# Causal masks of an attention's score maxima: two mask products that split the diagonal block by keys in place of queries

## The chip, the cores and the metric

The kernel runs on one core of one Trainium2 chip. The metric is device time in microseconds, from runs of the whole program, shown as a median with its lowest and highest value. One further execution is profiled; all rows below are from that one.

## The reference

Two layers on x of shape (2, 2048, 256). The first adds a differential attention and a mixture of experts, the second a state-space block and a sign-weight network. The change touches the attention alone:

```python
q, k, v = jnp.split(x @ w_attn, 3, axis=-1)       # 32 maps of 8 columns each, in pairs: 16 heads
att = jnp.einsum('bhtd,bhsd->bhts', q, k) * (1.0 / math.sqrt(hd))   # q scaled by hd ** -0.5 before
att = jnp.where(causal, att, -jnp.inf)
att = jax.nn.softmax(att, axis=-1)
att = att.reshape(B, H, 2, T, T)
att = att[:, :, 0] - lambda_full * att[:, :, 1]
out = jnp.einsum('bhts,bhsd->bhtd', att, v)       # then a norm, gamma and a projection
```

The softmax needs, for each query, the maximum over the keys up to and including its own.

## The kernel before

**Stages.** Norm, q/k/v and routing; the experts; the attention; the projection; the state-space and sign-weight stage. The tables of this change are made by GpSimd in the experts' stage (`phase_experts`, lines 782 to 791) and used in the attention's (`phase_attention`).

**Attention.** 32 heads (2 batches of 16), each with two maps a = 0 and 1. Map a has its q and k in rows 64a to 64a+63 of the slabs `qslab` and `kslab` (q and k are cut into bf16 parts, 48 rows in all), so a product of one map uses half of TensorE's rows and can run beside one of the other map. For each head there are

- 70 *maximum items* (`max_items`, numbered 0 to 69, even ones map 0, odd ones map 1). An item is one PSUM bank of up to 512 columns: products of 128 queries with up to 512 keys (L1374, `max_products`), for some a mask (L1388, `max_mask`), then one reduction on VectorE (L1322, `take_max`) into `pmax`. 48 items are full blocks of 512 keys. 22 are masked, since their last 128 keys are the queries' own (the diagonal block): items 2 and 3 hold four query tiles with 128 keys each; 8, 9, 14 and 15 hold two with 256 keys each; 22, 23, 28, 29, 34, 35, 40, 41, 46, 47, 54, 55, 60, 61, 66 and 67 hold one, with 384 or 512 keys.
- one transpose of the finished maxima (L1396), copied by ScalarE, cut by GpSimd into three bf16 rows and brought by DMA to rows 48 to 50 of `qslab`, so that the score product already subtracts the maximum.
- 40 *steps* of scores (L1426), exponentials on ScalarE (L1268), the causal cut on GpSimd where needed (L1200), and value products in f32 (L1441), which are issued for two steps at once.
- 4 *folds* (L1402): eight f32 records of 34 columns that sum the row groups.

**Order.** Items, transposes and folds share a ring of three PSUM banks, `psR`. Item number at in the ring may start only when what stood three places before it was read (`ring_free`). The order on every engine is written out: `place_items` spreads a head's items over the steps, most of them during the head before. TensorE takes all in program order, step by step: the first item's products, the two score products, that item's mask, the remaining fills, and at every second step the value products of two earlier steps. So whatever waits for a bank holds up all that is behind it.

**The mask.** It is added by accumulating products of `ident_b` (weights, rows to queries) with `mask_q` (0 or -1e30) onto the last 128 columns of each of the item's tiles. The items of one map may use 64 rows of the array only, so the 128 x 128 triangle takes two products of 64 rows. Before, product `part` adds the mask of queries 64 part to 64 part + 63, over all 128 keys: `ident_b[rows, part]` puts row r at query r + 64 part, and `mask_q[rows, part]` holds 128 keys. `mask_q` is read again for each tile of the item by a broadcast.

Of the kernel before, what the change touches and what calls it, by code (L numbers as in the profile page):

```python
# [6 lines left out]
BF16 = mybir.dt.bfloat16  # L7
# [4 lines left out]
ALU = mybir.AluOpType  # L12
AX = mybir.AxisListType

P = 128
# [15 lines left out]
NEG = -1e30  # L31
# [605 lines left out]
def phase_experts(nc, io, keep, dram):  # L637
# [4 lines left out]
    with ExitStack() as ctx:  # L642
# [3 lines left out]
        sem = lambda name: credited(ctx, nc, sems, name)  # L646
        MT = M // P
        HALF = P // 2
        SLABS = 2
        kslabs, qslabs = keep["kslabs"], keep["qslabs"]  # L650
        ident_b, mask_q, fold, lam_in, lam_s = (keep[x] for x in ("ident_b", "mask_q", "fold", "lam_in", "lam_s"))
# [69 lines left out]
        def _(sp):  # L721
# [22 lines left out]
            k_rows = dram["k"].rearrange("b n x d t -> (b n) x d t")  # L744
            sp.wait_ge(early_made, 2 * SLABS + 2 + CREDIT)
            for n in range(SLABS):
                for a in range(2):
                    row, lo = 2 * n + a, HALF * a
                    for at_, count, part in ((0, 3, 0), (3, 2, 1), (5, 1, 2)):
# [5 lines left out]
            for a in range(2):  # L755
                row, lo = a, HALF * a
                for at_, count, part in ((0, 3, 0), (3, 2, 1), (5, 1, 2)):
# [3 lines left out]
            for s in range(2):  # L761
                sp.wait_ge(y_out[s], 16 * (RT // 2) + CREDIT)
            for n in range(SLABS):
                sp.wait_ge(slab_in[n], 192 + CREDIT)

        @block.gpsimd
        def _(pool):
            c = Chain(pool, early_made)
            c.wait()
            for n in range(SLABS):  # L770
                for a in range(2):
                    c.mark(pool.memset(kslabs[n][HALF * a + 32:HALF * a + HALF, :], 1.0))
            c.wait()
            for a in range(2):
                c.after(pool.memset(qz[a][:], 0.0))
            c.after(pool.memset(ident_m[:], 0.0))
            c.after(pool.memset(mask_m[:], 0.0))
            c.after(pool.affine_select(out=ident_m[:], in_=ident_m[:], compare_op=ALU.not_equal, fill=1.0, base=0,
                                       pattern=[[-1, P]], channel_multiplier=1))
            c.after(pool.affine_select(out=mask_m[:], in_=mask_m[:], compare_op=ALU.is_ge, fill=NEG, base=0,  # L780
                                       pattern=[[-1, P]], channel_multiplier=1))
            c.after(pool.memset(ident_b[:], 0.0))
            c.after(pool.memset(mask_q[:], 0.0))
            c.after(pool.memset(fold[:], 0.0))
            for a in range(2):
                rows = slice(HALF * a, HALF * a + HALF)
                for part in range(2):
                    c.mark(pool.affine_select(out=ident_b[rows, part], in_=ident_b[rows, part], compare_op=ALU.not_equal,
                                              fill=1.0, base=HALF * part, pattern=[[-1, P]], channel_multiplier=1))
                    c.mark(pool.affine_select(out=mask_q[rows, part], in_=mask_q[rows, part], compare_op=ALU.is_ge,  # L790
                                              fill=NEG, base=HALF * part, pattern=[[-1, P]], channel_multiplier=1))
            c.wait()
            for odd in range(2):
                c.after(pool.affine_select(out=fold[:], in_=fold[:], compare_op=ALU.not_equal, fill=1.0,
                                           base=-VW * odd, pattern=[[-2 * VW, 2], [-1, OC]], channel_multiplier=1))
# [161 lines left out]
def phase_attention(nc, io, keep, dram):  # L957

    with ExitStack() as ctx:
# [23 lines left out]
        HALF = P // 2  # L983
# [3 lines left out]

        SLABS = 2
        ident_b, mask_q, fold, lam_s = (keep[x] for x in ("ident_b", "mask_q", "fold", "lam_s"))
# [368 lines left out]
        def _(pe):  # L1358
# [21 lines left out]
            def max_mask(n, x):  # L1380
                a, parts, masked = ITEMS[x]
                if not masked:
                    return
                w = parts[0][2]
                dst = psR[PLACE[("max", n, x)] % BANKS][:, 0:len(parts) * w].rearrange("p (m w) -> p m w", w=w)
                rows = slice(HALF * a, HALF * a + HALF)
                for part in range(2):
                    ins = pe.matmul(dst[:, :, w - P:w], ident_b[rows, part],  # L1388
                                    mask_q[rows, part].unsqueeze(1).to_broadcast([HALF, len(parts), P]),
                                    start=False, stop=(part == 1), skip_group_check=True)  # L1390
                ins.then_inc(ring_full, 1)

            def turn_max(n):
# [1090 lines left out]
def build(nc, io, out):  # L2484
    with ExitStack() as ctx:
# [13 lines left out]
        keep = {  # L2499
            "ident": sb(ctx, "ident", [P, P]),  # L2500
            "conv_w": sb(ctx, "conv_w", [P, CT, NTAP]),
            "vec": sb(ctx, "vec", [P, 3, CT]),
            "a_log": sb(ctx, "a_log", [P, CT, NS]),
            "a_neg": sb(ctx, "a_neg", [P, CT, NS]),
            "scal": sb(ctx, "scal", [P, 3]),
            "fac": sb(ctx, "fac", [P, 4]),
            "later_in": ctx.enter_context(nc.semaphore("later_in")),
# [5 lines left out]
        with ExitStack() as attn:  # L2513
            keep["c"] = sb(attn, "c_all", [P, NBLK, 2 * TPB])
            keep["yslot"] = sb(attn, "yslot_all", [P, NBLK, 2 * TPB], I32)
            keep["v"] = sb(attn, "v_all", [P, BATCH, HEADS, ST_T, VD])
            with ExitStack() as moe:
                keep["hot"] = sb(moe, "hot_all", [P, NBLK, 2, TPB, E])
                keep["slot"] = sb(moe, "slot_all", [P, NBLK, 2 * TPB])
                keep["table"] = sb(moe, "table", [P, 2, RT], I32)  # L2520
                keep["wg"] = sb(moe, "wg", [P, NE, KD, M])
                keep["wu"] = sb(moe, "wu", [P, NE, KD, M])
                keep["wd"] = sb(moe, "wd", [P, NE, M // P, D])
                phase_norm_qkv(nc, io, keep, dram)
                side = lambda name, shape, dt: early.enter_context(nc.sbuf_tensor(name, shape, dt, side="right"))
                keep["kslabs"] = [side(f"kslab{u}", [P, T], BF16) for u in range(2)]
                keep["qslabs"] = [side(f"qslab{u}", [P, T], BF16) for u in range(2)]
                keep["ident_b"] = side("ident_b", [P, 2, P], BF16)
                keep["mask_q"] = side("mask_q", [P, 2, P], BF16)
                keep["fold"] = side("fold", [P, 2, OC], F32)  # L2530
                keep["lam_in"] = side("lam_in", [P, 4, HD], F32)
                keep["lam_s"] = side("lam_s", [P, 2], F32)
                keep["pmax"] = side("pmax", [P, 2, ST_T, BPB], F32)
                keep["early_in"] = [early.enter_context(nc.semaphore(f"b_slab_in{u}")) for u in range(2)]
                phase_experts(nc, io, keep, dram)
            keep["o"] = sb(attn, "o_all", [P, NH, ST_T, VD])
            keep["raw_in"] = sb(attn, "raw_in", [P, ET, D])
            keep["raw_out"] = sb(attn, "raw_out", [P, KD, DI])
            keep["raw_x"] = sb(attn, "raw_x", [XD, DI])
            keep["raw_dt"] = sb(attn, "raw_dt", [P, CT, RANK])  # L2540
            keep["k0"] = sb(attn, "k0", [P, 2 * KD, F1], U8)
            keep["k1"] = sb(attn, "k1", [P, FT, F1], U8)
            keep["k2"] = sb(attn, "k2", [P, FT, D], U8)
            keep["wp"] = sb(attn, "wp", [P, KD, D])
            keep["gamma"] = sb(attn, "gamma", [P, 1])
            phase_attention(nc, io, keep, dram)
            early.close()
            keep["winT"] = far("winT", [P, KD, 2 * DI])
            keep["woutT"] = far("woutT", [P, CT, D])
            keep["wxT"] = far("wxT", [P, CT, XD])  # L2550
            keep["wdtT"] = far("wdtT", [RANK, DI])
            keep["w0"] = far("w0", [P, KD, F1], F16)
            keep["w1"] = far("w1", [P, FT, F1], F16)
            keep["w2"] = far("w2", [P, FT, D], F16)
            keep["skip"] = far("skip", [P, CT, P // 2])
            keep["taps"] = far("taps", [P, CT, NTAP, P])
            keep["xT"] = far("xT_s", [P, KD, BLK])
            keep["x1"] = far("x1_s", [P, TPB, D])
            phase_project(nc, io, keep, dram)
# [35 lines left out]
```

## Time and profile before

| | us |
|---|---|
| median of 3 runs | 3709.15 |
| lowest and highest | 3707.5, 3710.26 |
| profiled execution, its own time | 3713.02 |
| its span, from the first instruction to the last | 3711.3 |

The profile names engines PE (TensorE's products), PEld (its weight loads), DVE (VectorE), ACT (ScalarE) and POOL (GpSimd). A row of a group gives line, engine, operation, output and inputs, the shape, the count, busy time and the mean duration of one; then how long the engine had been idle before these instructions, and what ended it. The duration of one product runs until its last column has left the array, and the next product can follow before that, so durations overlap.

### The profile page before, as it was taken

How to read it: one execution, taken by the hardware profiler on the slowest of the kernel's cores; microseconds unless marked ns; L12 is line 12 of the kernel's file. 1: busy time of each engine (PE TensorE's matmuls, PEld its weight loads, DVE VectorE, ACT ScalarE, POOL GpSimd, SP SyncE). 2: the span in 40 equal slices, each digit the busy share in tenths (PEclk: the TensorE clock that was granted, in tenths of full speed). 3: DMA queues.
4: the chain of work that ended last, by engine and by line, in shares of the span. 5: the costliest groups of instructions: out<-in, count | busy, mean ns of one | idle time of the engine just before them, and what ended most of it. 6: DMA issues, size and time to landing. Idle time of an engine off the chain costs nothing. (4 is left out here: it accounts for less than half of the span.)

```text
span 3711.3 us, 61145 instructions
## 1 busy us (share of the span) xinstructions
PE 3425.7 (92%) x20658; PEld 1454.4 (39%) x20671; DVE 2739.1 (74%) x4434; ACT 2219.3 (60%) x3461; POOL 1499.4 (40%) x1843
## 2 busy tenths in 40 slices
PE   8996999989999999999999999767998998989987
PEld 5563666643333333333333333342333333333332
DVE  4653223468888888888888888265889888888888
ACT  3331221137777777777777777637767756667663
POOL 1212000013323333333233333215778777777786
PEclk9997999989999999999999999888999999999988
DMA  4443111111111011111100110031222222122221
GB/s 150 142 137 97 45 45 44 42 34 39 49 40 32 28 34 33 33 33 32 32 28 28 30 33 24 25 130 52 68 65 72 71 66 72 63 74 70 63 72 53
DMA packets 159224, 211.69 MB, mean 57 GB/s; under 512 B 30658, under 2 KB 106698, under 8 KB 158938
## 3 DMA queue, kind: packets, MB, share of 16 engines
q1 hardware_dynamic: 142042, 174.47, 15.6%
q10 hardware_dynamic: 10752, 16.78, 1.4%
q0 software_dynamic: 6144, 16.79, 1.4%
q8 instruction: 160, 2.62, 0.3%
q14 instruction: 126, 1.03, 0.1%
HBM read 154.48 MB, written 52.69 MB: 56 GB/s over the span
## 5 line engine op out<-in xcount | busy, mean ns | idle before, releaser
L1322 DVE TENSOR_REDUCE pmax<-psR 128x1 f32<-128x512 f32 (+3 forms) x2170 | 1321.5, 669 | 184.0 <-PE psR L1374 98.2
L1268 ACT ACTIVATE prob<-psS 128x1024 f32<-128x1024 f32 (+3 forms) x1280 | 1099.5, 904 | 364.2 <-PE psS L1426 360.8
L2081 POOL TENSOR_TENSOR hc<-h_d,crep 128x512 f32<-128x512 f32 x512 | 649.0, 1272 | 253.8 <-DVE h_d L2295 203.7
L1374 PE MATMUL psR<-kslab,qslab 48*128 48x512 bf16 (+3 forms) x2480 | 679.4, 353 | 38.7 <-DVE pmax L1322 10.9
L1426 PE MATMUL psS<-qslab,kslab 51*128 51x512 bf16 (+3 forms) x2560 | 646.7, 352 | 6.3 <-ACT prob L1268 4.3
L1441 PE MATMUL psVo<-prob,vaug 128*32 128x512 f32 (+3 forms) x5120 | 627.1, 545 | 0.9 <-ACT ov L1272 0.9
L1200 POOL TENSOR_SCALAR_AFFINE_SELECT prob<-prob 128x256 f32<-128x256 f32 (+1 forms) x512 | 208.8, 420 | 806.8 <-ACT prob L1268 806.5
L2295 DVE TENSOR_TENSOR_SCAN h_d<-a,state,psU 128x512 f32<-128x512 f32 x384 | 489.4, 1275 | 0.0
L2285 DVE TENSOR_TENSOR psU<-dtx,psX 128x512 f32<-128x512 f32 x512 | 356.1, 696 | 165.4 <-PE psX L2439 102.6
L1374 PEld LDWEIGHTS psR<-kslab,qslab 48*128 48x128 bf16 x2480 | 185.3, 94 | 726.2 <-DVE pmax L1322 512.6
L2203 ACT ACTIVATE a<-dt,a_neg 128x512 f32<-128x512 f32 x512 | 364.8, 720 | 54.5 <-DVE h_d L2295 53.1
L2456 PE MATMUL psYd<-hc,ident 64*64 64x512 f32 x2048 | 291.7, 641 | 7.9 <-POOL hc L2081 7.9
L2408 PE MATMUL psW<-f1h,w 128*128 128x512 f16 x512 | 195.4, 382 | 5.6 <-ACT xs L2134 3.9
L2408 PE MATMUL psW<-f1l,w 128*128 128x512 f16 x512 | 194.3, 380 | 0.0
L804 ACT ACTIVATE sg<-psG 128x512 f32<-128x512 f32 x72 | 43.0, 598 | 252.2 <-PE psU L896 252.2
L1173 POOL MEMSET kslab<- 32x2048 bf16 x4 | 7.2, 1798 | 461.8 <-SPq L1107 461.7
L1388 PE MATMUL psR<-mask_q,ident_b 64*128 64x512 bf16 (+1 forms) x1364 | 192.7, 241 | 0.0
L1426 PEld LDWEIGHTS psS<-qslab,kslab 51*128 51x128 bf16 x2560 | 158.2, 94 | 57.5 <-ACT prob L1268 33.9
L841 DVE COPY xT_e<-psX 128x256 f32<-128x256 f32 x72 | 30.3, 421 | 201.5 <-PE psX L883 201.5
L2295 DVE TENSOR_TENSOR_SCAN h_d<-a,psU 128x512 f32<-128x512 f32 x128 | 155.4, 1214 | 0.0
L275 POOL DMA_INDIRECT rows_d<-xn,slot x64 | 64.3, 1004 | 225.5 <-DVE slot L360 208.4
L1441 PEld LDWEIGHTS psVo<-prob,vaug 128*32 128x32 f32 x5120 | 102.3, 108 | 128.7 <-issue 88.6
(286 smaller groups left out, 4847.4 us busy)
## 6 DMA issues: line engine op xcount, KB each, us to landing
crep<-c_rows_d SPq DMA_DIRECT2D x256, 256.0 KB, 3.2
x_e<-rows_d SPq DMA_DIRECT2D x72, 128.0 KB, 2.0
y_d<-y SPq DMA_DIRECT2D x72, 128.0 KB, 1.7
q_d<-parts SPq DMA_DIRECT2D x48, 128.0 KB
k_d<-parts SPq DMA_DIRECT2D x48, 128.0 KB
qslab<-q_d SPq DMA_DIRECT2D x64, 96.0 KB
kslab<-k_d SPq DMA_DIRECT2D x64, 96.0 KB
x<-in_L_attn_x_dram SPq DMA_DIRECT2D x8, 512.0 KB, 6.0
```

The source lines that it names most:

```text
L1200: pool.affine_select(out=region, in_=region, compare_op=ALU.is_ge, fill=0.0, base=BLK * c + off - P * st, pattern=[[0, 2], [1, w]], channe ...
L1268: act.activation(prob[g % BUFS][:, :, off:BLK], psS[g % 2][:, :, off:BLK], ACT.Exp).then_inc(prob_ready, 1)
L1322: dve.tensor_reduce(pmax[:, a].rearrange("p i c -> p (i c)")[:, lo:lo + (count - 1) * NEXT + 1:NEXT], psR[at % BANKS][:, 0:count * w].rear ...
L1374: ins = pe.matmul(dst[:, m * w:(m + 1) * w], qslab[u][rows, i * P:(i + 1) * P], kslab[u][rows, ch * BLK:ch * BLK + w], start=(m == 0), sto ...
L1426: ins = pe.matmul(psS[g % 2][:, a, off:BLK], kslab[u][rows, st * P:(st + 1) * P], qslab[u][rows, c * BLK + off:(c + 1) * BLK], start=True, ...
L1441: ins = pe.matmul(psV[lo:lo + VW, off:BLK], vaug[n % 2][:, st, :], prob[g % BUFS][:, a, off:BLK], start=(st < 2), stop=(st >= TPB * c + TP ...
L2081: pool.tensor_tensor(hc[:, g % CR], h[:, g % HR], crep[:, g // PAIR % SPR], ALU.mult).then_inc(hc_ready, 1)
L2203: act.activation(a[:, g % AR], dt_[:, c], ACT.Exp, scale=a_neg[:, c, s:s + 1]).then_inc(a_ready, 1)
L2285: dve.tensor_tensor(psU[g % 2][:], dtx[:, c], psX[g // PAIR % 2][:], ALU.mult).then_inc(u_ready, 1)
L2295: dve.tensor_tensor_scan(h[:, g % HR], a[:, g % AR], psU[g % 2][:], 0.0 if blk % BPB == 0 else state[:, c, s:s + 1], ALU.mult, ALU.add).th ...
L2408: ins = pe.matmul(dst[:], ops[n][0], ops[n][1], start=(n == 0), stop=(n == OPS[kind] - 1))
L2456: ins = pe.matmul(psY[half][HALF * m:HALF * m + HALF, :], ident[rows, rows], hc[rows, (PAIR * k + m) % CR], start=False, stop=(s == NS - 1 ...
```

## The change

Each of the two products now covers 64 keys of a diagonal block in place of 64 queries. Product 0 adds the mask of keys 0 to 63: only queries 0 to 62 need one, row r for query r. Product 1 adds that of keys 64 to 127: row r for query r + 64 with r up to 62 (query 127 sees all keys), and the row that is left over, 63, masks all 64 keys for queries 0 to 63. So `mask_q` holds 64 keys for each part in place of 128, its row 63 of part 1 is -1e30 throughout, and `ident_b` has in row 63 of part 1 a one for queries 0 to 63 and a zero for query 127. Each product streams 64 columns for each tile in place of 128. Weights stay 64 rows of 128 columns, and the number of products stays. GpSimd makes the tables with six more selects, and with waits between them.

```diff
+        BIG = 1024
...
             for a in range(2):
                 rows = slice(HALF * a, HALF * a + HALF)
+                last = HALF - 1
                 for part in range(2):
-                    c.mark(pool.affine_select(out=ident_b[rows, part], in_=ident_b[rows, part], compare_op=ALU.not_equal,
-                                              fill=1.0, base=HALF * part, pattern=[[-1, P]], channel_multiplier=1))
+                    c.after(pool.affine_select(out=ident_b[rows, part], in_=ident_b[rows, part], compare_op=ALU.not_equal,
+                                               fill=1.0, base=HALF * part, pattern=[[-1, P]], channel_multiplier=1))
                     c.mark(pool.affine_select(out=mask_q[rows, part], in_=mask_q[rows, part], compare_op=ALU.is_ge,
-                                              fill=NEG, base=HALF * part, pattern=[[-1, P]], channel_multiplier=1))
+                                              fill=NEG, base=0, pattern=[[-1, HALF]], channel_multiplier=1))
+                c.wait()
+                c.after(pool.affine_select(out=ident_b[rows, 1], in_=ident_b[rows, 1], compare_op=ALU.is_ge,
+                                           fill=1.0, base=BIG * last - HALF, pattern=[[1, P]], channel_multiplier=-BIG))
+                c.after(pool.affine_select(out=ident_b[rows, 1], in_=ident_b[rows, 1], compare_op=ALU.not_equal,
+                                           fill=0.0, base=BIG * last + P - 1, pattern=[[-1, P]], channel_multiplier=-BIG))
+                c.after(pool.affine_select(out=mask_q[rows, 1], in_=mask_q[rows, 1], compare_op=ALU.is_ge,
+                                           fill=NEG, base=last - 1, pattern=[[0, HALF]], channel_multiplier=-1))
...
                 for part in range(2):
-                    ins = pe.matmul(dst[:, :, w - P:w], ident_b[rows, part],
-                                    mask_q[rows, part].unsqueeze(1).to_broadcast([HALF, len(parts), P]),
-                                    start=False, stop=(part == 1), skip_group_check=True)
+                    lo = w - P + HALF * part
+                    ins = pe.matmul(dst[:, :, lo:lo + HALF], ident_b[rows, part],
+                                    mask_q[rows, part].unsqueeze(1).to_broadcast([HALF, len(parts), HALF]),
+                                    start=False, stop=True, skip_group_check=True)
...
-                keep["mask_q"] = side("mask_q", [P, 2, P], BF16)
+                keep["mask_q"] = side("mask_q", [P, 2, P // 2], BF16)
```

## Rows read from the trace of the kernel before

**Rows 1.** Page, costliest groups of the whole span.

```profile
L1322 DVE TENSOR_REDUCE pmax<-psR 128x1 f32<-128x512 f32 (+3 forms) x2170 | 1321.5, 669 | 184.0 <-PE psR L1374 98.2
...
L1388 PE MATMUL psR<-mask_q,ident_b 64*128 64x512 bf16 (+1 forms) x1364 | 192.7, 241 | 0.0
```

**Rows 2.** Windows, ten heads: length, each engine's busy us, clock, DMA.

```profile
1000.00:1500.00 500.00, 485.89 (x4018) 175.09 (x4016) 438.45 (x739) 375.32 (x496) 157.53 (x315) 1.00 0.13 38
```

**Rows 3.** Waits in 1000 to 1500: us in all, times, longest.

```profile
PEld psR L1374 <- DVE pmax L1322: 167.0, 293, 0.8
...
ACT prob L1268 <- PE psS L1426: 113.3, 193, 1.1
...
DVE pmax L1322 <- PE psR L1374: 31.5, 92, 0.7
DVE pmax L1322 <- PE psR L1388: 27.1, 50, 1.0
```

**Rows 4.** Tile psR in 800 to 2300: min, median, max ns, first and last start.

```profile
L1396 PE MATMUL psR<-ident,nmax x30: 283/284/284, 844.2 to 2278.3; 128*32 128x128 f32 x30
```

**Rows 5.** Groups by form, PE, the masks' products of the whole span.

```profile
L1388 PE MATMUL psR<-mask_q,ident_b 64*128 64x128 bf16 x992 | 107.1, 216 | 0.0
...
L1388 PE MATMUL psR<-mask_q,ident_b 64*128 64x256 bf16 x248 | 48.0, 273 | 0.0
...
L1388 PE MATMUL psR<-mask_q,ident_b 64*128 64x512 bf16 x124 | 37.6, 383 | 0.0
```

**Rows 6.** Groups by form, weight loads in 1000 to 1500.

```profile
L1402 PEld LDWEIGHTS psR<-fold,ov 128*128 128x128 f32 x320 | 38.7, 191 | 14.6 <-issue 13.5
L1388 PEld LDWEIGHTS psR<-mask_q,ident_b 64*128 64x128 bf16 x442 | 37.2, 95 | 20.2
L1441 PEld LDWEIGHTS psVo<-prob,vaug 128*32 128x32 f32 x1624 | 32.2, 108 | 39.7 <-issue 27.0 <-ACT prob L1268 6.6
```

**Rows 7.** Timeline, items 22 and 23: start us, us, what [idle before it].

```profile
1401.42 0.22 PE L1388 MATMUL psR<-mask_q,ident_b 64*128 64x128 bf16 x1
...
1401.48 0.22 PE L1388 MATMUL psR<-mask_q,ident_b 64*128 64x128 bf16 x2
...
1401.73 2.82 DVE L1322 TENSOR_REDUCE pmax<-psR 128x1 f32<-128x384 f32 x5 [0.16 <-PE psR L1388]
```

**Rows 8.** Timeline, items 2 and 3 with the fold and the transpose.

```profile
1434.78 1.89 DVE L1322 TENSOR_REDUCE pmax<-psR 128x1 f32<-128x512 f32 x3
...
1434.89 0.59 PE L1388 MATMUL psR<-mask_q,ident_b 64*128 64x512 bf16 x2
...
1435.62 1.05 PE L1402 MATMUL psR<-fold,ov 128*128 128x34 f32 x8
...
1437.06 0.59 PE L1388 MATMUL psR<-mask_q,ident_b 64*128 64x512 bf16 x2
...
1437.58 0.28 PE L1396 MATMUL psR<-ident,nmax 128*32 128x128 f32 x1
1437.68 1.29 DVE L1322 TENSOR_REDUCE pmax<-psR 128x4 f32<-128x512 f32 x2 [1.01 <-PE psR L1388]
```

**Rows 9.** Timeline, items 8 and 9.

```profile
1440.19 0.38 PE L1388 MATMUL psR<-mask_q,ident_b 64*128 64x256 bf16 x2
...
1440.50 1.06 PE L1441 MATMUL psVo<-prob,vaug 128*32 128x512 f32 x8
...
1442.36 1.29 DVE L1322 TENSOR_REDUCE pmax<-psR 128x2 f32<-128x512 f32 x2 [0.66 <-PE psR L1388]
```

**Rows 10.** Timeline, item 35 and the value products behind it.

```profile
1408.88 0.27 PE L1388 MATMUL psR<-mask_q,ident_b 64*128 64x128 bf16 x2
1409.09 0.16 PEld L1441 LDWEIGHTS psVo<-prob,vaug 128*32 128x32 f32 x8
1409.09 1.06 PE L1441 MATMUL psVo<-prob,vaug 128*32 128x512 f32 x8
```

**Rows 11.** Timeline, load of a score product behind items 54 and 55.

```profile
1425.82 0.10 PEld L1426 LDWEIGHTS psS<-qslab,kslab 51*128 51x128 bf16 x2 [0.23 <-ACT prob L1268]
```

**Rows 12.** Timeline of GpSimd, the last mask select and what follows it.

```profile
326.79 0.29 POOL L790 TENSOR_SCALAR_AFFINE_SELECT mask_q<-mask_q 64x128 bf16<-64x128 bf16 x1
327.22 0.60 POOL L794 TENSOR_SCALAR_AFFINE_SELECT fold<-fold 128x34 f32<-128x34 f32 x2
```

## The prediction

> **What bounds the kernel now.** I read the page first. The masks' products at L1388 are 1364 records inside the attention stage, and the reductions they feed, L1322, are the largest group of the page [rows 1]. The question is whether that stage waits for TensorE. The windows view of 500 us in its middle gives PE 486 us busy, VectorE 438 and ScalarE 375 at a granted clock of 1.00 [rows 2]. "Busy" on PE includes the part of a product after its last column has entered, so 97% doesn't mean full. The waits of the same window say more: weight loads of the maxima's products wait 167.0 us for VectorE's reductions, and reductions wait 31.5 us for those products and 27.1 us (50 times) for the masks [rows 3]. So it is a ring of three PSUM banks in which now PE waits for VectorE, now VectorE for PE. ScalarE waits 113.3 us for scores, so it is rarely the bound. One head takes 49.45 us: 30 transposes of maxima start between 844.2 and 2278.3 us, 29 periods [rows 4]. The window holds ten heads, so VectorE waits five times a head for a mask, always at the same items, since the timeline repeats itself head by head.
>
> An average over waits does not tell what a shorter mask is worth, so I followed one head (1398.7 to 1448.1 us) through the timeline backwards: from a reduction that waited, to PE's product; along PE, until a product that itself began about 0.06 us after a reduction's end (a fold product 0.15 us after); along VectorE again. The saving counts only where that chain runs through a mask.
>
> **The change, part by part.**
>
> *The products.* There are 22 masked items a head, two products each: 16 items with one diagonal block, 4 with two, 2 with four. The streamed columns fall from 128, 256, 512 to 64, 128, 256. What a column costs: the record is 216, 273 and 383 ns [rows 5], about 0.43 ns a column on a fixed part; and one product follows the other in the same rows after 0.22 us at 512 columns (0.59 us for two less 0.38 for one), 0.11 at 256 (0.38 less 0.27), 0.06 at 128 (start 1401.42, then 1401.48) [rows 5, 7, 8, 9]. That is the streaming time and about 4 ns. So halving saves, for an item's two products: 2 x (0.217 - 0.110) = 0.21 us with four blocks, 2 x (0.110 - 0.057) = 0.107 with two, 2 x (0.057 - 0.030) = 0.054 with one. The first two go by paces that the trace shows. The 0.030 for 64 columns does not occur in it. Its bounds: 0.030 if streaming still sets the pace, 0.057 if something fixed (the weight load, which isn't shortened) does. The rows lean to 0.030: an f32 load of 128 columns is recorded at 191 ns and one of 32 at 108, thus 0.86 ns a column on 80 ns; the bf16 load is 95, which leaves 15 ns for the load proper [rows 6]. The fold's products show what such a load does when it sets the pace: eight in 1.05 us with some 0.28 for one is 0.11 us each for 34 columns, which is 128 x 0.86 ns [rows 8]. With 15 ns the load still hides under 27 ns of streaming. I take 0.030.
>
> The Trainium skill ("TensorE: Matmul & The Clock Gate", LDWEIGHTS) gives a load as columns / 1.2 ns, 107 ns for 128, and "it's the 128 columns that matter". By that, masks would go at 107 ns a product and the 64-column ones gain nothing. The trace contradicts it for bf16 (0.06 us a product with a load each) and agrees for f32 (0.11).
>
> *Which masks lie on the chain.* Item numbers are those of the list of 70.
> - Item 3 (four blocks). Mask to 1437.65, the transpose at 1437.58 right behind it, the values, then item 5's product; VectorE had stood 1.01 us for it [rows 8]. On the chain: 0.21.
> - Item 2 (four blocks). Its mask began at 1434.89, but the fold behind it started at 1435.62, 0.15 us after a reduction that freed its bank (the first of the three that start at 1434.78); by PE alone it could have started about 0.2 us earlier (the mask's streaming ends at 1435.32, and other products follow a mask 0.1 us behind it, as at item 35 [rows 8, 10]). VectorE sets it, so nothing: this 0.21 is lost.
> - Items 8, 9, 15 (two blocks). 8: the values start at 1440.50, right behind the second product; 9: VectorE stood 0.66 us for it [rows 9]; 15 as 8. 3 x 0.107 = 0.32.
> - One block: 22 (VectorE stood 0.16 us [rows 7]), 28 and 29 (side by side on the two halves of the rows, so once), 35 (values at 1409.09 right behind [rows 10]), 41, 66 and 67 (alike). 6 x 0.054 = 0.32, less 0.01 because VectorE had only about 0.09 us to spare at 67.
> - Items 54, 55: the chain behind them runs to a score product that waits 0.23 us for ScalarE [rows 11], whose work began ahead of these masks. Nothing.
> - The other eight (14, 23, 34, 40, 46, 47, 60, 61) end while VectorE has a backlog, and PE next waits for a bank. Nothing.
>
> Sum: 0.21 + 0.32 + 0.31 = 0.84 us a head. The first head's early items run alone before any scores, and the last head's period has no maxima, so 30 periods: 25 us. The waits allow this: VectorE stands (500 - 438) / 10 = 6 us a head [rows 2].
>
> *The set-up.* GpSimd gets six more selects of about 0.29 us and waits between them, some 2 us, after a last mask select at 326.79 [rows 12]. Nobody needs these tables before the attention stage, over 400 us on; GpSimd has only the fold's select behind them. In the path it would cost 2 us. The smaller mask tile moves its neighbours by 256 bytes, and both products now carry the stop flag: nothing.
>
> The sum against the profiled execution: 3713.0 - 25 = 3688. The median of the runs shown is 3.9 us below that execution, so 3709.15 - 25 = 3684 us.
>
> **Rivals.**
> 1. *The fixed part of a short product sets the pace (0.057).* One-block masks gain nothing, the others as above: 0.21 + 0.32 = 0.53 us a head, 16 us, 3693. For it: no 64-column product is in the trace, and both the load and the issue stay. Against: the load's 15 ns [rows 6]. The Trainium skill ("TensorEngine Tiling (Array Packing)", Instruction Overhead) has a floor of about 60 cycles a product, which 64 columns just clear; no row shows it.
> 2. *More than the chain.* Streamed time also helps where I wrote nothing: item 2, 54/55 and the backlog ones shift the pattern. All 22 would be 2 x 0.21 + 4 x 0.107 + 16 x 0.054 = 1.71 us a head, 52 us, 3657; with item 2 alone 1.05, 32 us, 3677. Against: PE waits for banks 167 us in 500, so most of what it gains off the chain it waits away.
> 3. *VectorE swallows it.* It is busy 438 of 500; if it gets a backlog earlier and the chain moves onto it, the saving returns as longer waits of PE for banks. Within 7 us if less than 0.24 us a head survives, about 3706. Against: at item 3 VectorE stands 1.01 us and at item 9 0.66, far above what is taken.
> 4. *Slower: unhidden loads.* If a load and its wait don't overlap a product this short, the pace could rise to the fold's 0.11 us. One-block items on the chain then lose 6 x 2 x (0.110 - 0.057) = 0.64 us, two-block ones gain nothing, item 3 keeps 0.21: +0.43 us a head, 13 us slower, 3722. It decides from a pace of about 0.10 us, where 12 x (pace - 0.057) passes 0.53. Against: two loads now follow at 0.06 us.
>
> **The numbers.** Forecast (gain 20 to 30 us) 0.52; rival 1 (10 to 20) 0.18; rival 2 (30 to 50) 0.17; rival 3 (under 7.4 either way) 0.09; rival 4 0.04. A difference of 0.2% (7.4 us) is about what a measurement can tell. Faster 0.87, same 0.09, slower 0.04. The range takes in rivals 1 and 2: 3660 to 3700.
>
> **What the changed profile would show.** Masks at 64, 128 and 256 columns with records near 188, 216 and 273 ns; two one-block products 0.03 us apart (rival 1: 0.06). Transposes of maxima 48.6 us apart in place of 49.45. VectorE's wait at item 3 near 0.8 us and at item 9 near 0.55; its waits on the masks down from 27.1 to about 22 us in 500. PE's waits for banks about as before (rival 3: up by what is saved). All other stages as long as now. I am wrong if the loads pace the short products, or if a place where I saw slack carries the chain once the masks before it are shorter.

## The result, and the profile after

Six runs of the changed kernel have a median of 3685.1 us (3683.3 to 3695.8), six of the kernel before 3709.7 us. The ratio is 0.9937, 95% interval 0.9927 to 0.9947: 20 to 27 us less. The prediction was 3684, 25 us less.

The profiled execution took 3683.5 us, its span is 3681.7. Lines have moved: products 1383, masks 1398, transpose of maxima 1406, folds 1412, scores 1436, values 1451, reductions 1331.

**The masks' products.** Groups by form on PE, whole span; they answer to [rows 5]:

```profile
L1398 PE MATMUL psR<-mask_q,ident_b 64*128 64x64 bf16 x992 | 87.3, 189 | 0.0
...
L1398 PE MATMUL psR<-mask_q,ident_b 64*128 64x128 bf16 x248 | 34.3, 218 | 0.0
L1398 PE MATMUL psR<-mask_q,ident_b 64*128 64x256 bf16 x124 | 24.0, 273 | 0.0
```

The same counts, half the columns; 189 ns is the 188 that the slope of [rows 5] gave. What matters is how closely they follow each other. The timeline of PE in the changed kernel, at items 22 and 23 as in [rows 7]:

```profile
1389.41 0.33 PE L1383 MATMUL psR<-kslab,qslab 48*128 48x384 bf16 x1
...
1389.57 0.19 PE L1398 MATMUL psR<-mask_q,ident_b 64*128 64x64 bf16 x1
...
1389.60 0.19 PE L1398 MATMUL psR<-mask_q,ident_b 64*128 64x64 bf16 x1
...
1389.63 0.22 PE L1398 MATMUL psR<-mask_q,ident_b 64*128 64x64 bf16 x2
```

Two products of item 22 start 0.03 us apart where 0.06 stood before, and the two of item 23 last 0.22 us together, 0.03 more than one. Start times are given to 0.01 us, so the 0.030 rests on both readings agreeing. It is what 64 columns at 0.42 ns and 4 ns of gap give: streaming still sets the pace, and the load stays hidden.

**The pace of a head.** Tile psR, transposes of maxima: count, min, median, max ns, first and last start. First the kernel before over its whole stage, then the changed one:

```profile
L1396 PE MATMUL psR<-ident,nmax x32: 283/284/372, 791.0 to 2325.7; 128*32 128x128 f32 x32
```

```profile
L1406 PE MATMUL psR<-ident,nmax x32: 284/284/372, 789.4 to 2298.9; 128*32 128x128 f32 x32
```

From first to last 1534.7 us became 1509.5: 25.2 us less over 31 periods. This length, called the *stage length* below, is the sharpest measure of the experiments, since noise elsewhere stays out of it. Each is read from one profiled execution; two kernels were profiled twice, and each pair agrees within 0.3 us. Within 1000 to 1500 us ten transposes start at 1042.0 to 1487.0 before and 1036.4 to 1473.9 after, so a steady head went from 49.44 to 48.61 us, 0.83 less; 0.84 was predicted.

**The waits.** The changed kernel, 1000 to 1500 us, answering to [rows 3]:

```profile
PEld psR L1383 <- DVE pmax L1331: 176.7, 303, 0.8
ACT prob L1277 <- PE psS L1436: 105.1, 185, 1.1
...
DVE pmax L1331 <- PE psR L1383: 31.3, 93, 0.7
...
DVE pmax L1331 <- PE psR L1398: 20.4, 41, 0.8
```

VectorE waits 6.7 us less for masks and as long as before for other products. The loads of the maxima's products wait 9.7 us more for VectorE, but that is mostly a change of label: the waits of the same loads that the profile puts under "issue" (nothing seen that they wait for) fell by 8.5. Before and after:

```profile
PEld psR L1374 <- issue: 60.0, 82, 0.8
```

```profile
PEld psR L1383 <- issue: 51.5, 73, 0.8
```

Nor is it what PE saves off the chain. The experiment e2 below, where only the masks on the chain are short, has the same two numbers (176.8 and 51.5); e3, where only the others are short, has 167.4 and 59.5, as before.

What PE saves at item 2 can be seen in one place. The fold behind it now shows a wait for VectorE, which it did not before:

```profile
1422.82 0.38 PE L1398 MATMUL psR<-mask_q,ident_b 64*128 64x256 bf16 x2
1423.55 1.05 PE L1412 MATMUL psR<-fold,ov 128*128 128x34 f32 x8 [0.35 <-DVE pmax L1331]
```

From the mask's start to the fold's it is 0.73 us, as in [rows 8] (1434.89 to 1435.62), though the mask is 0.21 us shorter.

**Item 3**, PE and VectorE in the timeline, answering to [rows 8]:

```profile
1424.99 0.38 PE L1398 MATMUL psR<-mask_q,ident_b 64*128 64x256 bf16 x2
...
1425.30 0.28 PE L1406 MATMUL psR<-ident,nmax 128*32 128x128 f32 x1
1425.41 1.29 DVE L1331 TENSOR_REDUCE pmax<-psR 128x4 f32<-128x512 f32 x2 [0.80 <-PE psR L1398]
```

From the start of the mask to the transpose it is 0.31 us in place of 0.52, and VectorE stands 0.80 us in place of 1.01. Both are the 0.21 of the sum.

### The profile page after: what moved, and what is told of

Read it like the earlier page. It is cut to its first block and busy times, and to the rows that moved or that the text cites. A ratio compares the mean times of both kernels' runs of the same rounds, so it can differ in the third digit from the quotient of the medians.

```text
span 3681.7 us, 61156 instructions
## 1 busy us (share of the span) xinstructions
PE 3381.3 (92%) x20658; PEld 1448.4 (39%) x20671; DVE 2735.0 (74%) x4434; ACT 2217.7 (60%) x3461; POOL 1501.7 (41%) x1849
## 5 line engine op out<-in xcount | busy, mean ns | idle before, releaser
L850 DVE COPY xT_e<-psX 128x256 f32<-128x256 f32 x72 | 30.3, 421 | 201.0 <-PE psX L892 201.0
L1412 PE MATMUL psR<-fold,ov 128*128 128x34 f32 x1024 | 136.0, 278 | 11.3 <-DVE pmax L1331 10.6
```

## The experiments

Each kernel is the changed one with one edit, run against the kernel before on the same chip. The stage length is read as above; the one of before is always that of its one profile (1534.7), which was not taken again beside the experiments. e1_wide, another execution that should equal it, is 0.1 away.

| kernel | median us | ratio to before, interval | stage length, us | less before's 1534.7 |
|---|---|---|---|---|
| changed | 3685.1 | 0.9937 [0.9927, 0.9947] | 1509.5 | -25.2 |
| e1_wide | 3712.7 | 1.0009 [0.9999, 1.0018] | 1534.8 | +0.1 |
| e2_on_chain | 3685.9 | 0.9938 [0.9921, 0.9954] | 1510.5 | -24.2 |
| e3_off_chain | 3710.9 | 1.0003 [0.9993, 1.0012] | 1534.0 | -0.7 |
| e4_item3 | 3702.3 | 0.9979 [0.9969, 0.9989] | 1528.3 | -6.4 |
| e5_four_of_32 | 3704.4 | 0.9984 [0.9974, 0.9993] | 1529.2 | -5.5 |
| e6_mask_first | 3679.1 | 0.9910 [0.9893, 0.9926] | 1504.2 | -30.5 |
| e7_no_masks | 3659.7 | 0.9857 [0.9840, 0.9873] | 1483.9 | -50.8 |
| e8_cut_22_28 | 3695.0 | 0.9963 [0.9950, 0.9976] | 1520.3 | -14.4 |
| e9_cut_rest | 3695.6 | 0.9961 [0.9946, 0.9977] | 1518.3 | -16.4 |
| after_again | 3684.5 | 0.9936 [0.9922, 0.9949] | 1509.2 | -25.5 |
| mask_first_again | 3677.5 | 0.9915 [0.9901, 0.9928] | 1504.4 | -30.3 |

**Which columns count: e1 to e4.** All four keep the changed kernel's split by keys, its stop flags and its way of making the tables. `mask_q` is 128 keys wide again, with zeros in the half that a product doesn't mask, so that a product can stream 64 keys or all 128 with the same result:

```diff
+        NARROW = (3, 8, 9, 15, 22, 28, 29, 35, 41, 66, 67)      # e2; e1: none; e3: the other 11; e4: (3,)
...
-                    lo = w - P + HALF * part
-                    ins = pe.matmul(dst[:, :, lo:lo + HALF], ident_b[rows, part],
-                                    mask_q[rows, part].unsqueeze(1).to_broadcast([HALF, len(parts), HALF]),
+                    at, cols = (HALF * part, HALF) if x in NARROW else (0, P)
+                    lo = w - P + at
+                    ins = pe.matmul(dst[:, :, lo:lo + cols], ident_b[rows, part],
+                                    mask_q[rows, part, at:at + cols].unsqueeze(1).to_broadcast([HALF, len(parts), cols]),
```

What was expected of e1, e2, e3 and e4, in this order:

> The new tables and the new split by keys, but every mask product streams all 128 keys of a diagonal block (64 of them against zeros). If the saving is the streamed columns on the chain, this is the kernel before: a head takes 49.45 us from transpose to transpose, the whole 3709 us, VectorE waits 27 us in 500 for the masks. If the split itself, the disjoint columns, the stop flags or the tables had part in it, it stays below, towards 48.6 us a head and 3685.

> Only the 11 items that the prediction put on the chain (3, 8, 9, 15, 22, 28, 29, 35, 41, 66, 67) stream 64 keys of a block, the other 11 stream 128. By the chain all of the gain is here: 48.6 us a head, 3685 us. If the gain is spread over all masks by their columns (rival 2), these 11 have 0.21 + 0.32 + 0.43 = 0.96 of 1.71 us, 56% of it: 0.5 of the measured 0.885 us, 48.95 us a head, 3695.

> Only the 11 other items (2, 14, 23, 34, 40, 46, 47, 54, 55, 60, 61) stream 64 keys of a block. By the chain nothing: 49.45 us a head, 3709 us, though PE streams 0.75 us less a head than before. Spread by columns: 0.39 us less, 49.06 us a head, 3697.

> Only item 3 (four blocks, map 1) streams 64 keys of a block. By the chain 0.21 us a head: 49.24 us, 6.4 us in all, 3703, VectorE's wait for it 0.80 in place of 1.01 us. If VectorE swallows it (rival 3): 49.45 and 3709.

Measured: e1 is the kernel before, so the split, the flags and the tables are worth nothing that shows; the saving is the streamed columns. e2 has 24.2 of the 25.2 us, e3 has 0.7. e4 has 6.4, what the chain gave for it (0.21 us x 31 is 6.5).

The two expectations for a spread by columns have a slip. The 11 items of e2 hold seven items with one block, not eight, so their share is 0.21 + 0.32 + 0.38 = 0.91 of 1.71 us, 53%, and PE streams 0.80 us less in e3, not 0.75; and the measured gain is 0.83 us a head, not 0.885. The spread would thus have given 13 us in e2 and 12 in e3. Neither is near what was measured.

In e3 the masks of 9 of the 16 one-block items and of items 2 and 14 are short, and VectorE still stands the full time at items 9 and 3, as these two groups show (VectorE by form, 1000 to 1500 us, e3):

```profile
L1333 DVE TENSOR_REDUCE pmax<-psR 128x2 f32<-128x512 f32 x40 | 26.6, 686 | 6.6 <-PE psR L1401 6.6
L1333 DVE TENSOR_REDUCE pmax<-psR 128x4 f32<-128x512 f32 x20 | 13.7, 687 | 10.2 <-PE psR L1401 10.2
```

Item 2's four blocks are narrow there and save nothing: the 10.2 us of standing, ten times at item 3, is that of the kernel before (10.2 in the same view; 8.0 in the changed kernel). Items 2 and 3 have the same columns; only where they stand in the order tells them apart. Item 3 was the only one of the eleven tried alone; how the other 18 us divide among the ten is the prediction's count.

**How short a product may be: e5, e8, e9.** The changed kernel with each product cut in two by keys, for all items (e5), for 22 and 28 (e8), for the other 20 (e9):

```diff
-                for part in range(2):
-                    lo = w - P + HALF * part
+                step = HALF // 2 if x in CUT else HALF
+                for at in range(0, P, step):
+                    lo, part, key = w - P + at, at // HALF, at % HALF
```

> The changed kernel with each mask product cut once more: four products of 32 keys a block in place of two of 64, the same columns in all, twice the weight loads. If streaming and some 4 ns set the pace down to here, a one-block product takes 13 + 4 = 17 ns, four take 0.07 us in place of 0.06, and the head stays within 0.2 us of 48.6; if a fixed floor of 30 ns stands behind the pace at 64 columns (load or issue), four one-block products take 0.12 us, 0.06 more an item, six times on the chain 0.36 us: 48.95 us a head, 3696; if the load of 57 ns came in, 0.17 more an item: 49.6 us a head, 3716.

e5 lost 19.7 us of stage length, 0.64 us a head: more than the floor of 30 ns gives (0.36), less than a load of 57. The timeline of PE has the pace:

```profile
1426.90 0.39 PE L1383 MATMUL psR<-kslab,qslab 48*128 48x512 bf16 x1
1427.13 0.25 PE L1399 MATMUL psR<-mask_q,ident_b 64*128 64x32 bf16 x4
```

Four products of 32 keys last 0.25 us, one alone 0.174 (its group's mean), so they follow at 0.025 us. Streaming would be 13 ns and 4 of gap: a fixed floor shows below 64 columns, and it is 25 ns, not 30 or 57. Two of 64 at 0.030 are 0.060, four at 0.025 are 0.100: 0.04 us an item, six times on the chain 0.24. The remaining 0.4 us a head came from a place that none of the expectations had, and the next two runs located most of it.

> The changed kernel, with the masks of items 22 and 28 alone cut into four products of 32 keys. With all 22 items so cut the stage grew by 19.7 us, 0.64 us a head. Theory: about half of that is here, because with four masks queued the product of the next item (23, 29), which uses the other half of the rows, no longer starts ahead of them: 0.35 to 0.45 us a head, 11 to 14 us. Rival: only the floor of 25 ns a product counts, everywhere alike: 2 x 0.04 = 0.08 us a head, 2.5 us.

> The changed kernel, with the masks of the other 20 items cut into four products. Theory: what is left of the 0.64 us a head, 0.2 to 0.3 us, 6 to 9 us. Rival (floor everywhere alike): 17 us.

e8 lost 10.8 us against the changed kernel, e9 8.8, together 19.6 of e5's 19.7. So two of the 22 items carry more than half: 0.35 us a head, of which the pace accounts for 2 x 0.04. That places 0.27 of the 0.4 us. The other 0.13 lie among the 20 items of e9 and were not placed. Timeline of PE in e8 at items 22 and 23, against that of the changed kernel above:

```profile
1394.64 0.18 PE L1400 MATMUL psR<-mask_q,ident_b 64*128 64x32 bf16 x1
1394.65 0.33 PE L1384 MATMUL psR<-kslab,qslab 48*128 48x384 bf16 x1
1394.67 0.22 PE L1400 MATMUL psR<-mask_q,ident_b 64*128 64x32 bf16 x3
...
1394.88 0.22 PE L1400 MATMUL psR<-mask_q,ident_b 64*128 64x64 bf16 x2
1395.03 0.63 PE L1453 MATMUL psVo<-prob,vaug 128*32 128x256 f32 x8
```

In the program the product of item 23 stands behind the masks of item 22. In the changed kernel it starts at 1389.41, 0.16 us *ahead* of them: it uses the other half of the rows, which is free, while the masks wait for a score product in their own half. In e8, with four masks queued ahead, it starts at 1394.65, just behind the first of them. So item 23's product and mask come 0.2 us late, and the value products with them: from item 22's product to the values it is 0.68 us (1394.35 to 1395.03) in place of 0.49 (1389.29 to 1389.78).

At items 28 and 29 the same happens. In the changed kernel item 29's product starts ahead of all masks, 0.23 us behind item 28's product, and the fold 0.54 us behind it:

```profile
1392.93 0.33 PE L1383 MATMUL psR<-kslab,qslab 48*128 48x384 bf16 x1
...
1393.16 0.32 PE L1383 MATMUL psR<-kslab,qslab 48*128 48x384 bf16 x1
1393.32 0.22 PE L1398 MATMUL psR<-mask_q,ident_b 64*128 64x64 bf16 x4
1393.47 0.97 PE L1412 MATMUL psR<-fold,ov 128*128 128x34 f32 x7
```

In e8 it is 0.40 us behind, after the first mask, and the fold 0.72:

```profile
1398.08 0.33 PE L1384 MATMUL psR<-kslab,qslab 48*128 48x384 bf16 x1
...
1398.47 0.18 PE L1400 MATMUL psR<-mask_q,ident_b 64*128 64x32 bf16 x1
1398.48 0.33 PE L1384 MATMUL psR<-kslab,qslab 48*128 48x384 bf16 x1
...
1398.80 1.08 PE L1414 MATMUL psR<-fold,ov 128*128 128x34 f32 x8
```

The two delays are 0.19 and 0.18 us here, and 0.17 each in the next head of both traces: 0.34 to 0.37 us a head. The stage grew by 0.35.

**What the masks still cost: e7.** The masks' products of heads 1 to 31 are left out; the maxima then go over keys that the causal mask excludes.

> Leaves out the masks' products of heads 1 to 31, so that the maxima go over the whole diagonal blocks, keys after the query too. What the masks still cost after the change: by their streaming on the chain as much again as was saved (0.84 us, since halving removed half), plus the hidden loads and the switch: 47.5 to 47.8 us a head, 3650 to 3661. If VectorE's own work is next, less is given: it is busy 43.3 us a head, so there is room.

Ten transposes start at 1032.9 to 1462.9 us, 47.78 us a head: 0.83 less than in the changed kernel, so beyond the streamed columns little shows. It takes another 25.6 us off the stage, as much as the change did (25.2). This run drops the weight loads and the gaps together with the remaining columns, so it doesn't part one from the other. The ten-head window gives VectorE 453 us busy, still 47 us idle, so it does not bound the whole period even there:

```profile
1000.00:1500.00 500.00, 477.74 (x3697) 149.38 (x3695) 452.93 (x766) 388.05 (x515) 162.34 (x321) 1.00 0.13 37
```

**A faster version: e6.** The step's first mask goes between the two score products:

```diff
-            def scores(g, order):
+            def scores(g, order, lead):
...
-                for a in order:
+                for n_, a in enumerate(order):
+                    if n_ == 1 and lead:
+                        max_mask(lead[1], lead[2])
...
-                    scores(g, (1, 0) if lead and ITEMS[lead[2]][0] == 0 else (0, 1))
-                if lead:
+                    scores(g, (1, 0) if lead and ITEMS[lead[2]][0] == 0 else (0, 1), lead)
+                elif lead:
```

> The changed kernel with the first item's mask issued between the two score products in place of behind both. VectorE gets a masked item 0.2 us earlier where such an item leads a step, and the second score product starts 0.06 to 0.21 us later. By the chain: a gain where the mask itself releases a VectorE that stands (9, 22, 28), nothing where the chain goes on to the values behind the scores, and ScalarE has room: 48.2 to 48.6 us a head, 3672 to 3685. The rival: ScalarE's exponentials come later, and the score waits behind them grow: above 48.6 us.

> The changed kernel itself, on the chip of the next one. Both theories: 0.9937 of the kernel before.

> The kernel with the first mask between the score products, as before. If its 5 us against the changed kernel are real: 0.992 of the kernel before, 3677 to 3682 us; if they were noise, 0.9937.

Stage length 5.3 us below the changed kernel the first time, 4.8 the second. On one chip, with five runs each, it is 3677.5 against 3684.5 us; the two intervals against the kernel before overlap a little (0.9901 to 0.9928, 0.9922 to 0.9949), so 7 us is a best estimate, while the stage length, shorter by about 5 us in both pairs, shows the order. VectorE in the timeline of mask_first_again, item 3 and then item 5:

```profile
1422.87 1.29 DVE L1331 TENSOR_REDUCE pmax<-psR 128x4 f32<-128x512 f32 x2 [0.58 <-PE psR L1383]
1424.61 0.69 DVE L1331 TENSOR_REDUCE pmax<-psR 128x1 f32<-128x512 f32 x1 [0.46 <-PE psR L1383]
```

and in the changed kernel at item 5:

```profile
1426.93 1.89 DVE L1331 TENSOR_REDUCE pmax<-psR 128x1 f32<-128x512 f32 x3 [0.24 <-PE psR L1383]
```

VectorE has item 3 0.22 us sooner (0.58 in place of 0.80) and stands 0.22 us longer at item 5 (0.46 in place of 0.24): given back in full, since PE goes from item 3 through the transpose and the values to item 5 in the same time as before. Item 9 keeps its share (same kernel and view):

```profile
1427.33 2.48 DVE L1331 TENSOR_REDUCE pmax<-psR 128x2 f32<-128x512 f32 x4 [0.23 <-PE psR L1398]
```

That is 0.23 us in place of 0.45 after the change; 4.8 to 5.3 us over 31 heads is 0.16 us a head, about this one item less small losses. VectorE's next wait behind it is as long as before (0.18 against 0.19 us), so nothing is given back there.

The expectation also named 22 and 28. At 22 the changed kernel's timeline shows no wait that could shrink. At 28 the wait of 0.23 us is gone, and the next one, at 1440.98, is 0.52 in place of 0.31: given back, as at item 3. At item 54 VectorE stands 0.31 us in place of 0.53, and at 59 0.38 in place of 0.22, so most of that is given back too.

## Why the prediction was right

**The size.** 0.84 us a head was predicted and 0.83 measured; over the stage 25.2 us, by the medians of the whole 24.6. The span of the two profiled executions differs by 29.6: by the rows above the stage begins 1.6 us earlier and what lies behind its last transpose is 2.8 us shorter. These are single executions. Over all 13 profiles the first transpose starts at 788.2 to 791.1 us, and 1381.5 to 1387.9 us lie behind the last, without relation to the masks; e1_wide, whose stage is that of before, begins at 789.9 and has 1381.7 behind it. So these 4 us need no cause in the change.

The prediction counted 30 periods, and there are 31 between the first transpose and the last: 30 x 0.83 is 24.9 us and 31 x 0.83 is 25.7, with 25.2 measured.

**The cost of a column.** The savings of 0.21 and 0.107 went by paces that the trace had, and item 3 alone measured 6.4 us. The unseen pace at 64 columns was put at 0.030 between 0.030 and 0.057, and is 0.030. Rival 1 is out. The argument from the load records ([rows 6], 15 ns for a bf16 load) pointed the right way. No run measures the 15 ns, which assume the same fixed 80 ns for bf16 as for f32; e5 shows that a load with its product fits into 25 ns, and that the pace goes no lower than this at 32 columns. Rival 4 is out by the same 0.030.

**The list of items on the chain.** e2 and e3 split the 22 as the prediction did: 96% of the gain is on one side, 3% on the other. Within the eleven only item 3 was tried alone, so the count of 28 and 29 as one, or the 0.01 taken off at 67, rests on reading the timeline. The three places where a saving was written off can be seen. Item 2: e3, and the fold's wait above. The backlog items: e3. Items 54 and 55: VectorE stands at 54 and at 59, before the change

```profile
1424.15 3.08 DVE L1322 TENSOR_REDUCE pmax<-psR 128x1 f32<-128x512 f32 x5 [0.58 <-PE psR L1388]
1427.40 1.29 DVE L1322 TENSOR_REDUCE pmax<-psR 128x1 f32<-128x512 f32 x2 [0.16 <-PE psR L1374]
```

and after it

```profile
1412.14 3.08 DVE L1331 TENSOR_REDUCE pmax<-psR 128x1 f32<-128x512 f32 x5 [0.53 <-PE psR L1398]
1415.44 1.29 DVE L1331 TENSOR_REDUCE pmax<-psR 128x1 f32<-128x512 f32 x2 [0.22 <-PE psR L1383]
```

The 0.05 us won at 54 is lost at 59, behind the score product that waits for ScalarE [rows 11]. Rival 2 (more than the chain) fell with e3. Rival 3 (VectorE swallows it) fell with the result itself, and e4 and e7 bear that out.

**What was read wrong, without changing the sum.** For item 9 the prediction expected VectorE to stand 0.55 us in place of 0.66. It stands 0.45 (the changed kernel's timeline of VectorE):

```profile
1429.87 3.18 DVE L1331 TENSOR_REDUCE pmax<-psR 128x2 f32<-128x512 f32 x5 [0.45 <-PE psR L1398]
```

PE goes through both item 8 and item 9 between VectorE's item 5 and item 9, so both savings of 0.107 show at one wait. The sum had both; the reading of one row took only the item's own. That is also most of why the waits on masks came to 20.4 us in 500, where 22 was expected.

Of PE's waits for banks about no change was expected. The row labelled VectorE grew by 9.7 us in 500 and the row labelled issue fell by 8.5, as shown above. Taken together they are 227.0 us before and 228.2 after, so the expectation holds for the sum and not for the one row.

**The set-up** ran as costed, on GpSimd with nobody waiting: the first of the two fold selects starts at 328.91 in place of 327.22 [rows 12], 1.7 us later (timeline of GpSimd, changed kernel).

```profile
328.91 0.60 POOL L803 TENSOR_SCALAR_AFFINE_SELECT fold<-fold 128x34 f32<-128x34 f32 x2 [0.21 <-POOL mask_q L799]
```

## What to carry to other kernels

Where two engines wait for each other in turn, neither the busy shares nor the total of waits price a change: follow one period backwards and count only what the chain passes through. Here 11 of 22 equal edits carried all of the gain, and twins (items 2 and 3) differed by everything. An earlier release of an engine that stands is worth something only if the chain goes on through that engine; if it goes on through the releasing engine, the same time comes back at the next wait (item 3 in e6). A row of waits that grows does not show by itself where a saving went: look at what the rows beside it did, and at runs with only part of the change. Halving the streamed columns paid in full here down to 64; cutting the products further cost time, most where it kept a product of the other row half from starting early.

## What the runs showed of the hardware that was not expected

- Bf16 products in the same rows, each with its own load of 128 columns, follow each other at 0.22, 0.11, 0.06 and 0.030 us for 512, 256, 128 and 64 columns (kernel before, changed kernel), but at 0.025 us, not 0.017, for 32 (e5).
- TensorE started a product of the other half of the rows 0.16 us ahead of two masks that stand before it in the program and waited for their own half (changed kernel, items 22 and 23). With four masks before it, it started behind the first (e8). Cutting the masks of two items a head so cost 10.8 us over 31 heads, about 8 of them beyond the slower pace (2 x 0.04 us a head). How far it looks ahead, and whether it counts products or their loads, was not tried.
